# Four residual layers on one core: per-group scaling and degree work on GpSimd, halved last norm, adjacent score halves, loads two groups ahead, own first and last orders

## The reference, cut to what matters

```python
h = einsum(adj, x @ W0 + b0) / adj.sum(-1)                       # layer 0
w = mask * rowdot(x @ Wq, adj @ (x @ Wk * mask)) / 16            # layer 1: one softmax per graph
y = softmax(w)[:, None] * (x @ Wv)
s = (q @ k.T) * HD**-0.5 * (adj + adj)                           # layer 2: 8 heads of 32
y = (softmax(s) @ v) @ Wo.T + bo
H = (adj != 0); Dn = 1/(H @ adj[0]); Be = 1/H.sum(0)             # layer 3
conv(x, W, b) = Dn * (H @ (Be * (H.T @ (x @ W.T)))) + b
y = conv(layernorm(relu(conv(x, W1, b1))), W2, b2) + x
```

## Time and profile before

| | us |
|---|---|
| median of 3 executions | 1965.06 (1964.87 to 1977.04) |
| the profiled execution: its own time | 1963.71 |
| its span, first to last instruction | 1962.0 |
| mean granted TensorE clock | 0.986 of full speed |

### The profile page before, as it was taken

How to read it: one execution, slowest core, us unless ns; L and a number is a source line. 1 busy time by engine, 2 the same in 40 slices (tenths; PEclk the granted TensorE clock), 3 DMA queues, 4 the chain that set the end, 5 groups by cost and what they waited for, 6 DMA issues and landing times.

```text
span 1962.0 us, 53573 instructions
## 1 busy us (share of the span) xinstructions
PE 1873.0 (95%) x15357; PEld 1630.5 (83%) x15357; DVE 1714.7 (87%) x4867; ACT 1478.6 (75%) x4431; POOL 1265.0 (64%) x2568
## 2 busy tenths in 40 slices
PE   5899999999999999999999999999999999999997
PEld 4788888888888888888888888888888888888886
DVE  5788988888988889888899888889888889888896
ACT  3677778777877777777777878777777778887775
POOL 1466766667765667566667666667666667666665
PEclk9899999999998999899999999999999999999999
DMA  3000000000000000000000000000000000000000
GB/s 112 2 28 28 5 21 27 27 27 27 5 21 27 27 27 21 6 27 27 27 27 7 20 27 27 27 27 8 19 27 27 27 27 5 21 27 27 27 11 12
DMA packets 57546, 46.14 MB, mean 24 GB/s; under 512 B 5168, under 2 KB 56880, under 8 KB 57520
## 3 DMA queue, kind: packets, MB, share of 16 engines
q1 hardware_dynamic: 55760, 43.93, 7.0%
q10 hardware_dynamic: 1760, 1.90, 0.3%
HBM read 29.04 MB, written 16.78 MB: 23 GB/s over the span
## 4 chain that ended last, share of the span: by engine, by line
PE 78%; DMA 5%; issue 5%; DVE 4%; POOL 4%; ACT 2%; SPq 1%; DVEq 0%; POOLq 0%; ACTq 0%
PE ps L340 38%; PE ps L403 7%; PE ps L443 6%; PE ps L411 6%; DMA a_in<-in_adj_dram 4%; PE ps L419 4%; PE ps L324 4%; PE ps L432 4%; PE ps L356 3%; PE ps L392 3%; POOL ln_rs L653 2%; PE ps L350 1%; DVE x2T L732 1%; PE ps L330 1%; ACT y_out L508 1%
## 5 line engine op out<-in xcount | busy, mean ns | idle before, releaser
L564 ACT ACTIVATE z<-z,z_max 128x128 f32<-128x128 f32 x1024 | 399.1, 398 | 7.2 <-DVE z_max L840 3.1
L653 POOL TENSOR_TENSOR ln_rs<-ln_ve,minus_half 128x1 f32<-128x1 f32 x640 | 360.8, 564 | 50.2
L674 POOL TENSOR_TENSOR z<-z,z_rcp 128x1024 f32<-128x1024 f32 x128 | 242.8, 1897 | 192.9 <-DVE z_rcp L847 192.9
L651 POOL TENSOR_TENSOR ln_ve<-ln_mv,eps_col 128x1 f32<-128x1 f32 x640 | 131.1, 205 | 192.7 <-DVE ln_mv L722 192.7
L656 POOL TENSOR_SCALAR ln_nm<-ln_mv,ln_rs 128x1 f32<-128x1 f32 x640 | 179.7, 281 | 109.8 <-POOL ln_rs L653 109.8
L829 DVE SCALAR_TENSOR_TENSOR z<-ps,a_hold 128x256 f32<-128x256 f32 x512 | 190.5, 414 | 61.4 <-PE ps L403 56.7
L340 PE MATMUL ps<-w1T,txT 128*128 128x512 f32 x768 | 205.0, 402 | 1.0 <-DVE txT L732 1.0
L340 PE MATMUL ps<-w2T,mnT 128*128 128x256 f32 x1536 | 202.3, 284 | 0.1
L564 ACT ACTIVATION_READ_ACCUMULATOR z<-z,z_max 128x1 f32 x1024 | 199.7, 195 | 0.0
L340 PEld LDWEIGHTS ps<-w2T,mnT 128*128 128x128 f32 x1536 | 185.6, 189 | 0.3 <-issue 0.3
L840 DVE TENSOR_REDUCE z_max<-z 128x4 f32<-128x512 f32 x256 | 172.3, 673 | 2.2
(11 more groups left out here) (149 smaller groups left out, 5092.4 us busy)
## 6 DMA issues: line engine op xcount, KB each, us to landing
x_in<-in_x_dram SPq DMA_DIRECT2D x32, 512.0 KB, 4.0
out_dram<-y_out SPq DMA_DIRECT2D x128, 128.0 KB, 1.7
a_in<-in_adj_dram SPq DMA_DIRECT2D x32, 256.0 KB, 2.8
...
```

Of the source, the lines that this page charges most:

```text
L564: m = act.activation(z[:, g % 2, h, :], z[:, g % 2, h, :], ACT.Exp, bias=z_max[:, g % 2, h:h + 1], accum_out=z_sum[:, g % 2, h:h + 1])
L651: pool.tensor_tensor(ve[n][:, g:g + 1], mv[n][:, g, 1:2], eps_col[:, :], ALU.add).then_inc(eps_made[n], 1)
L653: pool.tensor_tensor(rs[n][:, g:g + 1], ve[n][:, g:g + 1], minus_half[:, :], ALU.pow).then_inc(root_made[n], 1)
L674: pool.tensor_tensor(zg, zg, z_rcp[:, g % 2, :].unsqueeze(2).to_broadcast([P, HEADS, P]), ALU.mult)\
```

## The change: what it does

1. **POOL takes over** `mask`, `am` (one instruction for four graphs), `wm`, `hT` (the test for nonzero), `hb` (the scaling by the edge counts, one instruction for four), most of the degree steps (`dmax`, `dinv`) and, as two wide instructions for four graphs, the bias term `c3` that was `x3c` on DVE. One of the two `x3b` additions falls away. ACT takes over one small column copy (`hbc`).
2. **The last norm** works on half of its input: degree factors and `b2` are halved, `x3` is added once, and the norm uses a quarter of the epsilon.
3. **The hold copy** L877 goes; SP loads `a_hold` from memory, each graph's adjacency twice side by side, so that a half of the scores is scaled by one DVE instruction of 128x512.
4. **Loads** are one graph each (`lh`, `la`, `lx`), spread among the stores; `la` and `lx` are two groups ahead (`++`).
5. **Orders**: all lists are written anew; the first and last walks have lists of their own. Score halves stand next to each other more often. Each score half now waits for all four projections, not only the first of a group.
6. In layer 1 the factor 1/16 moves into the `gram` weights, the exponential is written in place in PSUM, and two small DVE steps go.

```diff
 ORDER_TEXT = {
     "pe": """
-        at.0+:3 at.1+:6 at.2+:2 sc0.0:0 mp.0:3 ax.0+:4 ax.1+:5 at.3+:7 sc1.0:2 v2.1:6 sc1.1:0 ax.2+:7
+        at.0+:5 at.1+:3 v2.1:4 sc1.0:0 sc0.0:6 v2.2:2 at.2+:0 ax.0+:3 sc1.1:1 mp.2:5 at.3+:0 ax.1+:3 h0.0+:4
...
     "sp": """
-        la.0+ lx.0+ store.0 store.1 store.2 store.3
+        lh.0+ la.0++ la.1++ store.0 la.2++ la.3++ lx.0++ lh.1+ lx.1++ store.1 lh.2+ lx.2++ lx.3++ store.2
+        lh.3+ store.3
...
-FIRST = {engine: [s for s in schedule if s[2] == 1] for engine, schedule in ORDER.items()}
-LAST = {engine: [s for s in schedule if s[2] == 0] for engine, schedule in ORDER.items()}
+ORDER, FIRST, LAST = ({engine: steps(text) for engine, text in texts.items()}
+                      for texts in (ORDER_TEXT, FIRST_TEXT, LAST_TEXT))
...
             def load_a(q, g):
 
-                after(sp, made["at"], q * G)
+                after(sp, made["at"], before(q, g, G))
                 after(sp, a_summed, q)
-                after(sp, a_held, q)
-                sp.dma_start(a_in[:, :, :], adj_d[bass.ds(q * G, G)].rearrange("g n m -> n g m")).then_inc(a_loaded, 16)
+                sp.dma_start(a_in[:, g, :], adj_d[bass.ds(q * G + g, 1)].rearrange("g n m -> n (g m)")).then_inc(a_loaded[g], 16)
+
+            def load_hold(q, g):
+
+                after(sp, read["sc0"], before(q, g, G))
+                after(sp, read["sc1"], before(q, g, G))
+                sp.dma_start(a_hold[:, g, :, :], adj_d[bass.ds(q * G + g, 1)].rearrange("g n m -> n g m").to_broadcast([P, C, P]))\
+                    .then_inc(hold_loaded[g], 16)
...
             def sc(half):
                 def stage(q, g, o, b):
-                    if g == 0:
-                        for s in ("q0", "q1", "k0", "k1"):
-                            pe.wait_ge(read[s], q + 1)
-                    for k in range(RG // 2):
-                        r = half * RG // 2 + k
-                        at_ = slice(r * HD, (r + 1) * HD)
-                        for c in range(C):
+                    for s in ("q0", "q1", "k0", "k1"):
+                        pe.wait_ge(read[s], q + 1)
+                    for c in range(C):
+                        for k in range(RG // 2):
+                            r = half * RG // 2 + k
+                            at_ = slice(r * HD, (r + 1) * HD)
...
+            def am(q, g):
+                pool.wait_ge(mask_made, q + 1)
+                pool.wait_ge(read["at"], nth(q, G - 1))
+                after(pool, made["amx"], q * G)
+                pool.tensor_tensor(amT[:, :, :], aT[:, :, :], mask[:, :].unsqueeze(2).to_broadcast([P, G, P]), ALU.mult)\
+                    .then_inc(amT_made, 1)
...
+            def hT_(q, g):
...
+                pool.tensor_scalar(hT[:, :, 0:P], aT[:, :, :], 0.0, 0.0, ALU.is_equal, ALU.is_equal).then_inc(hT_made, 1)
...
+            def hb_(q, g):
...
+                pool.tensor_tensor(hb[:, :, 0:P], hT[:, :, 0:P], e_rcp[:, :].unsqueeze(2).to_broadcast([P, G, P]), ALU.mult)\
+                    .then_inc(hb_made, 1)
...
+            def c3_(q, g):
+                pool.wait_ge(dcnt_made, q + 1)
+                after(pool, x3b_made, q * G)
+                pool.tensor_tensor(c3[:, :, :], bw_all[:, :].unsqueeze(1).to_broadcast([P, G, D]),
+                                   d_cnt[:, :].unsqueeze(2).to_broadcast([P, G, D]), ALU.mult).then_inc(c3_half, 1)
+                pool.wait_ge(c3_half, q + 1)
+                pool.tensor_tensor(c3[:, :, :], c3[:, :, :], b2_all[:, :].unsqueeze(1).to_broadcast([P, G, D]), ALU.add)\
+                    .then_inc(c3_made, 1)
...
-                pool.tensor_tensor(x3b[:, g, :], x3[:, g, :], b2_all[:, :], ALU.add).then_inc(x3b_half, 1)
-                pool.wait_ge(x3b_half, nth(q, g))
-                pool.tensor_tensor(x3b[:, g, :], x3b[:, g, :], x3[:, g, :], ALU.add).then_inc(x3b_made, 1)
...
+                pool.tensor_tensor(x3b[:, g, :], x3[:, g, :], c3[:, g, :], ALU.add).then_inc(x3b_made, 1)
...
+            def z_(half):
+                def run(q, g, o):
...
+                    dve.scalar_tensor_tensor(out=z[:, g % 2, hs, :].rearrange("p (r c) n -> p r (c n)", r=RG // 2),
+                                             in0=ps[:, b:b + RG // 2, 0:C * P], scalar=HC,
+                                             in1=a_hold[:, g, :, :].rearrange("p c n -> p (c n)").unsqueeze(1)
+                                             .to_broadcast([P, RG // 2, C * P]),
+                                             op0=ALU.mult, op1=ALU.mult).then_inc(read[f"sc{half}"], 1)
...
-            def hold_a(q, g, o):
-                dve.wait_ge(a_loaded, q * 16 + 16)
-                after(dve, read["sc0"], q * G)
-                after(dve, read["sc1"], q * G)
-                dve.tensor_copy(a_hold[:, :, :], a_in[:, :, :]).then_inc(a_held, 1)
```

More of the change, by code:

```diff
@@ L541, in aT_free @@
                 after(act, made["ax"], before(q, g, G))
-                after(act, amT_made, before(q, g, G))
+                after(act, amT_made, q)
                 after(act, hT_made, q)
-                after(act, cnt_made, q * 2)
+                after(act, col_made, q)
             def mp_free(q, g):
@@ L557, in wt, with hbc, attn @@
                 act.wait_ge(p_bias_made, q + 1)
-                act.activation(e_row[0:G, :], o[0:G, 0:P], ACT.Exp, bias=w_stat[0:G, 1:2], scale=INV,
-                               accum_out=w_stat[0:G, 2:3]).then_inc(read["wt"], 1)
-            def attn(q, g, part):
-                act.wait_ge(max_made[part], nth(q, g))
-                for h in range(part * HEADS // 2, (part + 1) * HEADS // 2):
+                act.activation(o[0:G, 0:P], o[0:G, 0:P], ACT.Exp, bias=w_stat[0:G, 0:1],
+                               accum_out=w_stat[0:G, 1:2]).then_inc(p_exp_made, 1)
+            def hbc(q, g, o):
+                act.wait_ge(read["at"], nth(q, G - 1))
+                after(act, made["mp"], q * G)
+                act.copy(hb[:, :, P:P + 1], aT[:, :, 0:1]).then_inc(col_made, 1)
+            def attn(q, g, half):
+                act.wait_ge(max_made[half], nth(q, g))
+                for h in range(half * HEADS // 2, (half + 1) * HEADS // 2):
                     m = act.activation(z[:, g % 2, h, :], z[:, g % 2, h, :], ACT.Exp, bias=z_max[:, g % 2, h:h + 1],
                                        accum_out=z_sum[:, g % 2, h:h + 1])
-                m.then_inc(exp_made[part], 1)
+                m.then_inc(exp_made[half], 1)
             def pt(q, g, o, b):
@@ L604, in _, with walk @@
             }
-            def walk(schedule, it):
-                for stage, g, ahead, _ in schedule:
+            def walk(orders, it):
+                bank = BANKS_OF[id(orders)]
+                for stage, g, ahead, _ in orders["act"]:
                     q = it + ahead
                     if stage == "pt":
-                        pt(q, g, None, BANK["pt", g])
+                        pt(q, g, None, bank["pt", g])
                     elif stage in ("exp0", "exp1"):
@@ new lines, in wm_ @@
+            def wm_(q, g):
+                pool.wait_ge(mask_made, q + 1)
+                pool.wait_ge(read["xg"], nth(q, G - 1))
+                after(pool, made["wt"], q)
+                pool.tensor_tensor(wm[:, :], w[:, :], mask[:, :], ALU.mult).then_inc(wm_made, 1)
+            def hT_(q, g):
+                pool.wait_ge(set_ident, 1)
+                pool.wait_ge(read["at"], nth(q, G - 1))
+                after(pool, made["mp"], q * G)
+                after(pool, cnt_made, q)
+                pool.tensor_scalar(hT[:, :, 0:P], aT[:, :, :], 0.0, 0.0, ALU.is_equal, ALU.is_equal).then_inc(hT_made, 1)
@@ L737, in asum @@
             def asum(q, g, o):
-                dve.wait_ge(a_loaded, q * 16 + 16)
-                after(dve, wm_made, q)
-                dve.tensor_copy(mask[:, :], maskT[:, bass.ds(q * G, G)]).then_inc(mask_made, 1)
+                for k in range(G):
+                    dve.wait_ge(a_loaded[k], q * 16 + 16)
                 dve.tensor_reduce(a_sum[:, :], a_in[:, :, :], AX.X, ALU.add).then_inc(a_summed, 1)
@@ L821, in sc, with drcp @@
-            def sc(half):
-                def run(q, g, o, b=None):
-                    b = BANK[f"sc{half}", g]
+                dve.wait_ge(cnt_made, q + 1)
+                dve.reciprocal(e_rcp[:, :], e_cnt[:, :]).then_inc(ercp_made, 1)
+            def drcp(q, g, o):
+                dve.wait_ge(dmax_made, q + 1)
+                after(dve, dhalf_made, q)
+                dve.reciprocal(d_rcp[:, :], d_max[:, :]).then_inc(drcp_made, 1)
+            def z_(half):
+                def run(q, g, o):
```

343 lines of the change are left out of this document (199 added, 144 removed).

## The result

| | us |
|---|---|
| changed kernel, median of 4 executions | 1863.28 (1862.67 to 1865.63) |
| kernel before, measured beside it, 4 executions | 1964.87, 1965.06, 1977.04, 1986.92 |
| ratio | 0.944, 95% interval 0.938 to 0.951 |
| profiled execution of the changed kernel: own time, span | 1865.63, 1863.9 |

The forecast was 1890, with 1848 to 1940 as its range. Against 1965.1 us, the time that the forecast started from, the change takes 102 us off, 5.2%; against all four executions of the kernel before beside it, as in the ratio, 5.6%.

What follows compares the result with a forecast made beforehand. PE was taken as the bound, with small gaps in each turn. From 1963.7 us, score pairs -38 + 6, loads -22, clock -12 and ends -8 sum to -74: 1890 us, range 1848 to 1940.

Steps and rivals of the forecast that it cites:

- (a): Other gaps in PE's turn, 0.6 us, close as well, and both ends give 16 instead of 8: 1857 us; 15%.
- What bounds the kernel: In the loop, PE sets the pace, busy 57.25 of 58.84 us a turn; DVE would be next.
- Adjacent halves, -38 + 6 = -32: PE's score halves: three adjacent pairs a turn instead of one save 38 us; repeated projection waits cost 6.
- Loads, -22: Head of the turn: loading two groups ahead removes PE's 21.9 us of waits for the adjacency.
- clock, -12: Three loop stretches at low clock, some 4 us each, go if the load gap before them is filled.
- First and last lists, -8: Before and behind the loop, own lists close part of the idle time: 8 us, bounds 0 to 26.
- DVE to POOL, 0: Work moved from DVE to POOL adds nothing to the sum, since neither engine is the bound.
- `c3` fits with about 1 us to spare: POOL before the first graph's `ln3` root: 6.1 us until `mn.0` may start, against 7.0 of PE work.
- rival (b): POOL comes late at `mn.0` and something similar at a `probs`, about 1.5 us a turn: 1936 us; 14%.
- (c): Adjacent score halves bring nothing, PE's sequencer being the bound there: +32, 1922 us; 12%.
- (d): Gap at the turn's head grows and the low clock comes in most turns, 4 us each: 2014 us; 6%.
- (e): A `hold` or `x` load late each turn and POOL late too: all but the pairs eaten, 1955 to 1965; 6%.

Runs made afterwards that it cites:

- e8_pairs_split: The changed kernel with the two new pairs of score halves in a turn taken apart again in PE's list: 1890.44 us, turn 57.22.
- e2: The changed kernel with all loads back to one group ahead and behind the four stores: 2092.08 us, ratio 1.055 to the kernel before.

## Why the prediction was right, point by point

The side and the range were right; the forecast lay 27 us too high. Of the cases, (a) came nearest: its 1857 stood on 0.6 us a turn of further gaps and 16 us at the ends, and both are there. Its third term, 6 us, was given no reason, and the cause of the gaps, the loads themselves, was not in it, so its nearness is partly luck.

**What bounds the kernel**, PE's own work and gaps: right. 56.1 of 56.5 us in a turn are PE.

**Adjacent halves, -38 + 6 = -32**: measured 27. The mechanism was right. That the size was nearly right is partly luck, since two errors cancel: PE's busy time in the scores fell by 0.59 us a turn and not 1.2, because the two new pairs take 1.17 and 1.05 us; 0.2 of each is the repeated waits (forecast 0.18, half of the time), and 0.26 and 0.12 more over the 0.70 stay without them, with the later start of the second half. Another 0.2 us a turn came from gaps. What was not foreseen is that the 0.2 us of the waits is worth nothing once removed, since bank 0 ties the head of the turn.

**Loads, -22, and clock, -12**: measured 59 together. This is the term that made the forecast too high. The wait row of PE's matmuls holds 0.73 us a turn; the turn gave back 1.47. The row of its weight loads already held 0.94, and the features' load, which the sum left out, held the first `ax` back by 0.48 on average. The clock term was right for this execution: 14 against 12. That the kernel before took up to 1994 us elsewhere says that three low stretches are no fixed number.

**First and last lists, -8**: 13.7 to 16.5. Taken too near to nothing.

**DVE to POOL, 0**: the sum still closes: 59 + 27 + 16.5 = 102.5 of 101.8 us, so about nothing is left for all other parts together. But this is a balance of differences taken partly from the old order and partly from the new one, not a row of zeros. The halved norm and the shorter steps of layer 1 have no run of their own. The hold copy alone gives 11 in the old order, and with `am` and `hb` back on DVE the new order loses 51. The step that failed is "relief of DVE alone gives nothing directly": DVE at 80% of a turn holds PE wherever something that PE waits for stands behind a blocked instruction. The Trainium skill's sentence quoted against this part (Perfetto Trace Analysis, Optimizing Scalar/DVE Operations), that moving work between the two engines might not help, did not decide it here: for `am` and `hb` together the move gave 51 us, and it took `am` on DVE from beside a wide POOL instruction.

**`c3` fits with about 1 us to spare**: 0.4. The second product took 2.40 us where 1.90 was used, which is 0.5 of the missing 0.6. The experiment with 1.9 us more is rival (b) made real: 1929 us, where 1936 was worked out for it, with 0.9 us at `mn.0` and 0.6 elsewhere where 1.5 and 0.5 were found.

**A turn of 56.5 us** was measured (56.4), but it didn't follow from the sum: -54 us over 32 turns gives 57.1. The missing 0.7 us is the load term's, so that this number was right by luck.

**Rivals.** (c), pairs bring nothing: refuted by e8_pairs_split. (d), the low clock: not in the changed kernel; e2 shows that it would have come, and dearer (7.6 us a turn, the wait included, against the 4 used) with late loads. (e): no.

**Signs named.** No `a_in` wait, no low clock, DVE and POOL loads: as said. "L481 x16 of 0.7 to 0.8": wrong for two of three. And one sign of a wrong forecast did appear, the second half of a pair 0.2 us or more behind for issue (0.46 and 0.37), though the pairs still paid.
